# Four waited one-row memsets on GpSimd after every eighth record scatter and every eighth gather of the first edge loop, in an eight-layer graph network

## The reference, cut to what matters

```python
h = x @ W
s = h @ a[:f_out]
t = h @ a[f_out:]
logit = s[src] + t[dst]
e = jnp.exp(-jax.nn.leaky_relu(logit, ALPHA))
rowsum = jax.ops.segment_sum(e, src, num_segments=n)
h_prime = jax.ops.segment_sum(e[:, None] * h[dst], src, num_segments=n) / rowsum[:, None]
return jax.nn.relu(h_prime)
```

## Time and profile before

| | us |
|---|---|
| median of 3 runs | 5627.28 |
| lowest and highest | 5613.48, 5653.24 |
| the profiled execution's own time | 5643.58 |
| its span | 5641.8 |
| PE busy | 3893.5 (69%) |
| DVE busy | 3225.1 (57%) |
| ACT busy | 2676.4 (47%) |
| POOL busy | 2550.5 (45%) |

### The profile page before, as it was taken

The page is one execution under the profiler, slowest core; times in us unless marked ns, Lnnn a source line. Parts: engine busy times, 40 slices in busy tenths (PEclk is TensorE's granted clock), DMA queues, the critical chain, the costliest instruction groups (busy, mean ns, idle before and its releaser), DMA issues.

```text
span 5641.8 us, 74245 instructions
## 1 busy us (share of the span) xinstructions
PE 3893.5 (69%) x19152; PEld 2563.7 (45%) x19152; DVE 3225.1 (57%) x8314; ACT 2676.4 (47%) x8902; POOL 2550.5 (45%) x2689
## 2 busy tenths in 40 slices
PE   3177788882243899997866666667899974665665
PEld 1023565661232444445744444444556543444454
DVE  4178466651324789987666777774333344555653
ACT  3065366661121788885433655564333324555522
POOL 5702555555434777760524555542000036666334
PEclk7588799885576899998988888888999986777778
DMA  3001322240222333341244555551000013333334
GB/s 111 11 11 40 83 76 76 76 78 10 63 87 68 85 85 88 90 84 65 71 128 143 143 144 145 144 143 53 1 12 12 15 57 83 88 89 87 47 108 129
DMA packets 278820, 441.37 MB, mean 78 GB/s; under 512 B 114083, under 2 KB 192781, under 8 KB 278157
## 3 DMA queue, kind: packets, MB, share of 16 engines
q0 software_dynamic: 124624, 331.70, 23.2%
q1 hardware_dynamic: 147230, 98.37, 6.0%
q10 hardware_dynamic: 6560, 6.55, 0.4%
HBM read 368.84 MB, written 67.60 MB: 77 GB/s over the span
## 4 chain that ended last, share of the span: by engine, by line
PE 44%; DVE 17%; another core or an unknown queue 17%; issue 11%; ACT 7%; DMA 2%; DVEq 2%; POOL 1%; ACTq 0%; SPq 0%; POOLq 0%
PE PB L3163 6%; PE PB L2005 5%; PE PB L726 4%; PE PB L2539 4%; PE PB L1076 4%; PE PB L3147 3%; ACT XNT L2623 3%; PE PB L2015 2%; DVE bigt L705 2%; PE PB L1085 1%; PE PB L1571 1%; PE PB L1559 1%; PE PB L2027 1%; PE PB L2022 1%
## 5 line engine op out<-in xcount | busy, mean ns | idle before, releaser
L2539 PE MATMUL PB<-XNT 128*128 128x260 f32 x1760 | 631.0, 495 | 168.6 <-DVE bigt L2511 90.8
L1020 POOL DMA_INDIRECT bigt<-HTAB,bigt x440 | 420.2, 955 | 554.8 <-DMA HTAB<-bigt 231.6
L726 PE MATMUL PB<-bigt 128*128 128x440 f16 x1564 | 392.6, 372 | 286.8 <-ACT bigt L717 123.1
L717 ACT ACTIVATE bigt<-bigt 128x128 f16<-128x128 f16 x1214 | 382.7, 389 | 400.8 <-remote 213.0
L2657 POOL DMA_INDIRECT bigt<-ZTAB,DO x440 | 456.6, 1038 | 227.1 <-issue 111.9
L1977 POOL DMA_INDIRECT bigt<-YTAB,bigt x440 | 475.9, 1082 | 176.1 <-issue 127.7
L705 DVE TENSOR_SCALAR bigt<-PB,bigt 128x440 f16<-128x440 bf16 x782 | 313.7, 437 | 345.5 <-remote 187.5
L2539 PEld LDWEIGHTS PB<-XNT 128*128 128x128 f32 x1760 | 384.7, 241 | 251.8 <-issue 141.9
L359 POOL DMA_INDIRECT RECS<-bigt x391 | 379.0, 969 | 155.4 <-issue 118.9
L2623 ACT ACTIVATE XNT<-bigt 128x65 f32<-128x65 f32 x1768 | 446.3, 336 | 0.0
L2005 PE MATMUL PB<-bigt 128*128 128x512 f32 x880 | 405.4, 603 | 3.0 <-DVE bigt L2197 3.0
(11 more groups left out here) (490 smaller groups left out, 9386.1 us busy)
## 6 DMA issues: line engine op xcount, KB each, us to landing
bigt<-YTAB,bigt POOLq DMA_INDIRECT x552
bigt<-SRT SPq DMA_DIRECT2D x56, 128.0 KB
OUTS<-bigt SPq DMA_DIRECT2D x56, 128.0 KB
SRT<-bigt SPq DMA_DIRECT2D x11, 640.0 KB, 9.8
bigt<-HTAB,bigt POOLq DMA_INDIRECT x440
bigt<-ZTAB,DO POOLq DMA_INDIRECT x440
KVTAB<-bigt SPq DMA_DIRECT2D x25, 258.0 KB, 2.3
YTAB<-bigt SPq DMA_DIRECT2D x10, 640.0 KB, 10.3
```

The lines of the kernel that those rows point to most:

```text
L717: m = e.activation(self.L[:, c % self.RB, k, :], self.lanes[:, b % 2, j, :], ACT.Copy, scale=self.N2[:, c, k:k + 1])
L726: m = e.matmul(PB[self.acc[k]][:, 0:self.chunks], self.L[:, c % self.RB, k, :], self.R[:, c % self.RB, :], start=(c == 0), stop=(c == EC - 1))
L1020: e.indirect_dma_start(out=Gt[:, g % GB, j, :], out_offset=None, in_=HTAB, in_offset=bass.IndirectOffsetOnAxis(ap=SO[:, g * G + j:g * G + ...
L2539: m = e.matmul(self.PV[n % len(self.PV)], self.OH[:, g % self.MB, j, :], self.msg[:, g % self.MB, j, :], start=(k == 0), stop=(k == self.H ...
```

## The change

A helper `rest` is added and called in two places. It issues a memset of one partition by 128 elements on POOL and waits for it, four times. `iotai` is read by nothing after the first stage. It is called after every eighth attribute scatter (columns 7, 15, ..., 383: 48 times, of them 23 in the first sort, 9 in the 78, 11 in the 85 and 5 in the last 43) and after the last gather of each odd group of the first edge loop (55 times). Nothing else moves.

```diff
+        def rest(e):
+
+            for _ in range(4):
+                e.memset(iotai[0:1, :].bitcast(FP), 0.0).then_inc(Q.up(), 1)
+                e.wait_ge(*Q.now())
+
@@ attr_scatters
                 e.indirect_dma_start(
                     out=RECS, out_offset=bass.IndirectOffsetOnAxis(ap=APOS[:, c:c + 1].bitcast(U32), axis=0),
                     in_=ATTR[:, piece % 2, k, :], in_offset=None).then_inc(recs_out[piece % 2].sem, 16)
+                if c % 8 == 7:
+                    rest(e)
                 recs_next[0] = c + 1
@@ pool_edges
                             in_offset=bass.IndirectOffsetOnAxis(ap=SO[:, g * G + j:g * G + j + 1].bitcast(U32), axis=0),
                         ).then_inc(gathered.sem(g), 16)
+                    if g % 2:
+                        rest(e)
```

## The result

| | us |
|---|---|
| before, median of 4 (lowest, highest) | 5636.39 (5613.48, 5653.24) |
| after, median of 4 (lowest, highest) | 5553.91 (5511.81, 5562.82) |
| ratio, 95% interval | 0.9851 (0.982 to 0.9882) |
| profiled execution of after, its span | 5562.82, 5561.1 |

The change makes the kernel 1.5% faster, 82 us where 440 were forecast. The lines of the kernel after stand 6 lines further down in the scatters (L365), 8 in the first edge loop (L1028 gathers, L713 and L734 are the sort's L705 and L726), and 10 behind it (L1742 is L1732, L1987 is L1977). The memset of a rest is L346.

The account below looks back on a forecast made before the run. The prediction took the kernel to be held by PE's updates delayed behind POOL's unbroken indirect DMAs. Savings of 188 + 70 + 80 + 77 + 25 = 440 us off 5643.6 gave 5204, forecast as 5187 for the median; range 5110 to 5450.

Parts of the forecast that it names:

- What bounds the kernel: First sort: PE's semaphore updates wait while POOL issues indirect DMAs every 1.27 us and something takes 1.39 us for each.
- What a rest costs POOL: Each rest of four waited memsets behind POOL's transfers: 0.61 us for the first, 1.32 for three more, together 1.9 us.
- The lower bound of 1.0: Least cost of a rest on POOL, in us: the waits alone, 4 times 0.24.
- Whether it is enough: Runs of eight transfers: POOL gains 1.0 us, a rest of 1.9 gives it back, spacing becomes 1.51 us, stall goes.
- The bounds of 209 and 172 us: First sort: range of the saving, for a rest of 1.0 or 2.6 us.
- First sort: First stage until gathers begin: unstalled sort ends near 295 us, POOL's scatters with rests at 334.8; 188 us saved.
- Edge loop: First edge loop's gathers: 14.0 us for two groups becomes 12.6, over some 51 pairs; 70 us saved, bounds 0 and 100.
- End of the edge loop: From the last gather to ACT's scaling, beside 78 scatters: 130 us become 50; 80 us saved, bounds 50 and 90.
- third layer: 43 scatters with 5 rests end 9.5 us later, POOL's 34.5 us wait goes; 25 us saved, bounds 0 and 30.
- Expert layer: Until the first gather back: 238 us become 161, with POOL the bound by 10 us; 77 us saved, bounds 55 and 85.
- The first rival: Stall thinner but stays, as a queue needs a pause longer than 1.9 us: 5300 to 5520, middle 5407; chance 0.14.
- The second to fourth: Rivals: rests miss the cause, 5718 us, chance 0.06; a rest is long, 5700, 0.04; no effect, 5627, 0.06.

Follow-up runs that it names:

- e6: The kernel before, unaltered, run for its profile on a chip with the stall: 5578.14 us in its one execution.
- e7: Eight waited memsets in each rest where the changed kernel has four, on a chip with the stall: 5208.91 us, ratio 0.9349 to the kernel before.
- e13: The kernel of e7 again, as base of a later set on a chip with the stall: 5196.59 us, ratio 0.9347 to the kernel before.
- e1: Eight memsets in each rest where the changed kernel has four, on the chip without the stall: 4877.86 us, ratio 1.0462 to the kernel before.
- e10: Sixteen memsets after each 32nd transfer where the changed kernel has four after each eighth, on a chip with the stall: 5470.69 us, ratio 0.9821 to before.

## Why the prediction was wrong, point by point

- **What bounds the kernel: right.** The late updates are what holds the first sort: POOL's DMAs are the same in e6 and e7, only their spacing isn't, `moved` comes 0.32 us late instead of 3.85, and DVE is busy 94.81 us of 100 instead of 9.83. That the sort's stall comes from a server of 1.39 us a transfer fits the spacings; what the server is remains open, except that it isn't the DMA engines, which are done 22 us before the tail ends.
- **What a rest costs POOL: the step that failed.** 0.96 us and not 1.9. It was put together from the copy in the earlier trace rows, 0.86 us between two gathers for 0.45 of work. That excess isn't paid by a memset, which starts where the DMA ends. And 0.24 from the earlier trace rows isn't the wait behind a memset: it is the idle time before another kind of instruction. In a rest the trace has 0.20 of work and 0.06 between two memsets, so each further one costs 0.25 where the sum had 0.44. The lower bound of 1.0 was the value by luck: it counted that 0.24 four times and left out the work.
- **Whether it is enough: wrong at that bound.** "Even the lower bound just does" took the point at which the backlog stops growing for the point at which the stall ends. At 1.39 the backlog is indeed gone (3 us of tail for 24), and DVE gets 21 us of 100. It takes 1.46 for 87 and 1.51 for 95. The bounds of 209 and 172 us for the first sort should therefore have reached down to about 30 at a rest of 1.0 us.
- **First sort, 188:** 177 in e7, 30 in the change (522.8 to 493.2).
- **Edge loop, 70:** 23 in e7. The pace with rests was right, 12.6 us a pair against 12.5 in e7 and 12.3 in e13. The start was mis-sized: it was read from one place, 14.0; over the whole loop of before it is 742.5/55 = 13.5, and in e6 12.9. The 3.9 us of waiting in it stand in none of the lines of the earlier trace rows.
- **End of the edge loop, 80; third layer, 25:** 77 and 24 in e7, and 8 and 2 in the change.
- **Expert layer, 77:** 53 in e7; 184 us where 161 was worked out. POOL was to be the bound by 10 us, and it still waits 21.3 us for the slots' results. In e1, without the stall, it waits for them not at all and the stretch takes 163.3 us, so what was mis-sized is the stall that is left in the slots' loop.
- **The first rival** was the case that came true, at 5554 beyond its end of 5520. It gave a queue that needs a longer pause as the reason. The pause was half as long as that rival took it to be, and e10 shows that one of 4 us gives no more at the same mean spacing. It deserved more than 0.14. The second to fourth fall: the rests reach the cause, are short, and do something.
- **The page of the Trainium skill** ("DMA: Bandwidth & Descriptors"), whose figure gave an estimate of 1.6 us a transfer: 1.51 us already frees the engines (e7), and 1.39 clears the backlog, so the runs speak against that figure taken 16 times in a row.

## What to carry to other kernels

When one engine issues small transfers back to back and all others slow down with "remote" as releaser, compare two times: the spacing of the issues, and the time from the first issue until the others are free, divided by the number of transfers. If the second is longer, slow the issuer until its spacing is clearly above it, not equal to it; here 5 to 9% above did it (1.46 and 1.51 against 1.39). Where the issuer has little waiting of its own to give up, as in the ZTAB layer, the pauses cost more than they bring. Price a filler by its whole period in a row, and take the lower bound as a case of its own when the effect has a threshold near it. And try such a change on more than one chip: where the stall is absent every rest is paid in full.

## What the runs showed of the hardware that was not expected

- **Chips differ by 19% on this kernel**: before takes 4661 us on one and 5561, 5571 and 5566 on three others (medians of seven). On the first the rests of eight memsets cost 4.6%, on two of the others they gain 6.5%. The first sort is the plain sign, DVE 100.00 (e1) against 9.83 us of 100 (e6). What differs between the chips no run shows, nor whether it is the chip or the state it was in, since each was used for one set.
- **The stall goes with missing records**: the traces with the stall hold about half as many records of semaphore updates (31,354 in the kernel before, 31,678 in e7) as those without it (63,167 in e1, which is e7's kernel). An untested rival follows from this: recording the updates may itself be what takes the time. Every time here is of an execution whose clock was recorded, so no run tells what the kernels take unrecorded.
- **A waited one-row memset on POOL takes about 0.24 us**, in chains of 2 to 16 (0.45, 0.95, 1.45, 1.96 and 3.97 us), also right behind an indirect DMA.
- **The clock follows**: in the same window of the sort the granted clock is 0.50 (1.2 GHz) in e6, with PE busy 14.69 us of 100, and 1.00 (2.4 GHz) in e7, with 83.79.
